# New order tables for the five engines of a one-core decoder layer

## The reference

```python
x = x + _L0_attn_ref(_layernorm(x, axis=-1), Wq, bq, Wk, bk, Wv, bv, Wo, bo)      # causal, with ALiBi
x = x + _L0_xattn_ref(_layernorm(x, axis=-1), ctx_1024, ctx_1024, ...)            # cross attention
x = x + _L0_ffn_ref(_layernorm(x, axis=-1), weight, aux_weight1, aux_weight2, bias)
# attention: softmax(q k^T / 4 + bias) v, then the output projection
# ffn: tanh(h @ weight @ aux_weight1 @ aux_weight2 + bias)
```

## Time and profile before

| | |
|---|---|
| median of 3 runs | 2504.38 us (2502.93 to 2504.84) |
| profiled execution | 2503.5 us, its span 2501.8 us |
| PE, busy of the span | 2335.8 us (93%) |
| PEld | 1856.7 us (74%) |
| DVE / ACT / POOL | 1700.1 (68%) / 1384.2 (55%) / 717.8 us (29%) |
| granted TensorE clock, mean | 0.984 |
| DMA | 244.83 MB, mean 98 GB/s |

### The profile page before, as it was taken

How to read it: one execution, slowest core, us unless ns; L and a number is a source line. 1 busy time by engine, 2 the same in 40 slices (tenths; PEclk the granted TensorE clock), 3 DMA queues, 4 the chain that set the end, 5 groups by cost and what they waited for, 6 DMA issues and landing times.

```text
span 2501.8 us, 67273 instructions
## 1 busy us (share of the span) xinstructions
PE 2335.8 (93%) x22072; PEld 1856.7 (74%) x22072; DVE 1700.1 (68%) x3710; ACT 1384.2 (55%) x3066; POOL 717.8 (29%) x1371
## 2 busy tenths in 40 slices
PE   4799999999999999999999999999999999999995
PEld 3677777777777777777777777777777777777763
DVE  4477667767767767767767767776776776776752
ACT  2455555565565555555555555556556556556551
POOL 3132233233233233233222223223223323323321
PEclk9899999999999999999999999999999999999995
DMA  8333433443343343333343343344344334334320
GB/s 157 88 101 96 110 97 85 107 112 86 104 112 83 101 106 93 105 103 85 101 107 93 101 107 93 89 107 104 90 107 105 85 100 113 92 100 109 86 69 21
DMA packets 167370, 244.83 MB, mean 98 GB/s; under 512 B 22176, under 2 KB 90512, under 8 KB 164248
## 3 DMA queue, kind: packets, MB, share of 16 engines
q1 hardware_dynamic: 165660, 244.22, 37.4%
q10 hardware_dynamic: 1664, 0.01, 0.1%
HBM read 53.13 MB, written 33.56 MB: 35 GB/s over the span
## 4 chain that ended last, share of the span: by engine, by line
PE 53%; DVE 11%; DMA 10%; issue 9%; ACT 8%; POOL 4%; SPq 4%; ACTq 0%; DVEq 0%; POOLq 0%
PE ps_misc L540 14%; PE ps_score L614 7%; PE ps_misc L526 6%; PE ps_attend L639 5%; DMA k_stack<-k_nat 5%; DMA q_stack<-neg_max_t_s 5%; DVE neg_max_s L954 4%; PE ps_misc L669 4%; PE ps_misc L510 3%; PE ps_score L615 3%; PE ps_max L597 3%; ACT xprobs L804 3%; PE ps_score L624 2%; DVE chain_t L937 2%; PE ps_attend L643 2%
## 5 line engine op out<-in xcount | busy, mean ns | idle before, releaser
L797 ACT ACTIVATE probs<-ps_score 128x384 f32<-128x384 f32 x1024 | 468.6, 494 | 113.3 <-PE ps_score L615 111.1
L954 DVE TENSOR_REDUCE neg_max_s<-ps_max 128x2 f32<-128x512 f32 (+1 forms) x768 | 478.7, 678 | 8.4 <-PE ps_max L585 4.4
L804 ACT ACTIVATE xprobs<-ps_score 120x512 f32<-120x512 f32 x512 | 280.7, 603 | 222.9 <-PE ps_score L624 222.8
L1080 POOL TENSOR_SCALAR ve_LN<-mv_LN 128x2 f32<-128x2 f32 x192 | 36.8, 191 | 1213.6 <-DVE mv_LN L976 1213.6
L614 PE MATMUL ps_score<-q_stack,k_stack 128*128 128x256 f32 x1024 | 353.2, 351 | 27.6 <-DMA q_stack<-neg_max_t_s 13.9
L962 DVE TENSOR_REDUCE neg_max_x<-ps_max 128x4 f32<-128x480 f32 x512 | 313.8, 649 | 61.1 <-PE ps_max L597 61.1
L615 PE MATMUL ps_score<-q_stack,k_stack 128*128 128x256 f32 x1024 | 283.8, 281 | 0.0
L614 PEld LDWEIGHTS ps_score<-q_stack,k_stack 128*128 128x128 f32 x1024 | 193.9, 189 | 109.3 <-ACT probs L797 47.1
L624 PE MATMUL ps_score<-xq_stack,xk_stack 128*120 128x256 f32 x1024 | 228.6, 316 | 6.6 <-DMA xq_stack<-neg_max_t_x 2.8
L1106 POOL TENSOR_TENSOR res<-res,chain_n 128x512 f32<-128x512 f32 x64 | 82.5, 1288 | 442.9 <-ACT chain_n L842 442.9
L597 PE MATMUL ps_max<-xk_stack,xq_stack 127*128 127x120 bf16 x2048 | 195.3, 220 | 1.2 <-DVE neg_max_x L962 1.2
(11 more groups left out here) (147 smaller groups left out, 5365.2 us busy)
## 6 DMA issues: line engine op xcount, KB each, us to landing
k_stack<-k_nat SPq DMA_DIRECT2D x192, 256.0 KB, 3.6
q_stack<-q_nat SPq DMA_DIRECT2D x192, 256.0 KB, 3.7
xq_stack<-q_nat SPq DMA_DIRECT2D x192, 256.0 KB, 3.6
xk_stack<-scr_xk SPq DMA_DIRECT2D x192, 128.0 KB, 2.9
x_in<-in_x SPq DMA_DIRECT2D x64, 256.0 KB, 2.8
scr_xk<-k_nat SPq DMA_DIRECT2D x32, 512.0 KB, 3.4
out_y<-res SPq DMA_DIRECT2D x64, 256.0 KB, 2.2
ctx_in<-in_ctx SPq DMA_DIRECT2D x32, 240.0 KB, 4.1
```

The lines of the kernel that those rows point to most:

```text
L797: act.activation(probs[:, h % 8, :], bank_of("SCORE", i, b, h)[:, P:4 * P], ACT.Exp)\
L804: act.activation(xprobs[0:C, at:at + 2, :], blocks(bank_of("XSCORE", i, b, u))[0:C], ACT.Exp).then_inc(sem("xprobs_ready"), 1)
L954: dve.tensor_reduce(o, ins, AX.X, ALU.max, negate=True).then_inc(sem("max_taken"), 1)
```

## The change

New tables for SP, PE, ACT, DVE and POOL in ORDER. They hold the same tasks, begun at another point of the cycle (PE's old table begins at SCORE 11 of the sequence in self attention, the new one at SCORE 4), with some moved: XK, XQ, LN2_T, V, XMAX, MAX, FFN and OUT_PROJ among others. Three functions follow: after_first is called on each engine before its first task that comes_first doesn't name, and no longer at t == 0; the wait of other_weights on PE covers all tasks done before it; and XHEADS_OUT of the last sequence on DVE waits for out_ready (cross_free). END_STEP is one lower.

```diff
--- before.py
+++ after.py
@@ -64,51 +64,50 @@
 
 ORDER = {
     "SP": (
-        ("STORE", -3, 0), ("XMAX_STACK", -2, 0), ("LOAD_X", 1, 0), ("XK_STACK", -1, 0),
-        ("MAX_STACK", 0, 0), ("XQ_STACK", -1, 0), ("LOAD_CTX", 0, 0),
-        ("K_STACK", 1, 0), ("Q_STACK", 1, 0), ("XK_SAVE", 0, 0),
+        ("LOAD_X", 1, 0), ("MAX_STACK", 0, 0), ("XK_STACK", -1, 0), ("LOAD_CTX", 0, 0),
+        ("XQ_STACK", -1, 0), ("K_STACK", 1, 0), ("Q_STACK", 1, 0), ("XMAX_STACK", -1, 0),
+        ("STORE", -2, 0), ("XK_SAVE", 0, 0),
     ),
     "PE": (
-        ("SCORE", -1, 11), ("ATTEND", -1, 1), ("SCORE", -1, 12), ("SCORE", -1, 13),
-        ("LN3_T", -3, 0), ("XMAX", -2, 3), ("ATTEND", -1, 2), ("SCORE", -1, 14), ("XMAX", -2, 4),
-        ("SCORE", -1, 15), ("XMAX", -2, 5), ("FFN", -3, 0), ("ATTEND", -1, 3), ("XMAX", -2, 6),
-        ("V", 0, 0), ("XMAX", -2, 7), ("HEADS_OUT", -1, 0), ("HEADS_OUT", -1, 1), ("MAX", 0, 0),
-        ("XMAX_T", -2, 0), ("MAX", 0, 1), ("OUT_T", -1, 0), ("MAX", 0, 2), ("XV", -1, 0),
-        ("MAX", 0, 3), ("MAX", 0, 4), ("MAX", 0, 5), ("OUT_PROJ", -1, 0), ("XSCORE", -2, 0),
-        ("XSCORE", -2, 1), ("MAX", 0, 6), ("MAX", 0, 7), ("XSCORE", -2, 2), ("MAX", 0, 8),
-        ("XSCORE", -2, 3), ("XATTEND", -2, 0), ("XSCORE", -2, 4), ("MAX", 0, 9), ("XSCORE", -2, 5),
-        ("XATTEND", -2, 1), ("MAX", 0, 10), ("XSCORE", -2, 6), ("MAX", 0, 11), ("XSCORE", -2, 7),
-        ("LN2_T", -1, 0), ("MAX_T", 0, 0), ("XATTEND", -2, 2), ("XATTEND", -2, 3), ("XQ", -1, 0),
-        ("SCORE", 0, 0), ("SCORE", 0, 1), ("XHEADS_OUT", -2, 0), ("SCORE", 0, 2),
-        ("XHEADS_OUT", -2, 1), ("SCORE", 0, 3), ("LN1_T", 1, 0), ("SCORE", 0, 4), ("XOUT_T", -2, 0),
-        ("ATTEND", 0, 0), ("SCORE", 0, 5), ("K", 1, 0), ("SCORE", 0, 6), ("XOUT_PROJ", -2, 0),
-        ("SCORE", 0, 7), ("SCORE", 0, 8), ("CTX_T", 0, 0), ("Q", 1, 0), ("SCORE", 0, 9),
-        ("XMAX", -1, 0), ("SCORE", 0, 10), ("XMAX", -1, 1), ("XK", 0, 0), ("XMAX", -1, 2),
+        ("SCORE", 0, 4), ("ATTEND", 0, 0), ("SCORE", 0, 5), ("XOUT_T", -2, 0), ("SCORE", 0, 6),
+        ("K", 1, 0), ("SCORE", 0, 7), ("SCORE", 0, 8), ("XOUT_PROJ", -2, 0), ("SCORE", 0, 9),
+        ("Q", 1, 0), ("XMAX", -1, 0), ("SCORE", 0, 10), ("SCORE", 0, 11), ("XMAX", -1, 1),
+        ("ATTEND", 0, 1), ("SCORE", 0, 12), ("XMAX", -1, 2), ("CTX_T", 0, 0), ("SCORE", 0, 13),
+        ("XMAX", -1, 3), ("XMAX", -1, 4), ("XMAX", -1, 5), ("SCORE", 0, 14), ("LN3_T", -2, 0),
+        ("XMAX", -1, 6), ("SCORE", 0, 15), ("XK", 0, 0), ("XMAX", -1, 7), ("ATTEND", 0, 2),
+        ("FFN", -2, 0), ("XMAX_T", -1, 0), ("MAX", 1, 0), ("MAX", 1, 1), ("ATTEND", 0, 3),
+        ("MAX", 1, 2), ("MAX", 1, 3), ("MAX", 1, 4), ("HEADS_OUT", 0, 0), ("MAX", 1, 5),
+        ("HEADS_OUT", 0, 1), ("XSCORE", -1, 0), ("XSCORE", -1, 1), ("MAX", 1, 6), ("XV", 0, 0),
+        ("OUT_T", 0, 0), ("XATTEND", -1, 0), ("XSCORE", -1, 2), ("XSCORE", -1, 3), ("MAX", 1, 7),
+        ("MAX", 1, 8), ("MAX", 1, 9), ("XSCORE", -1, 4), ("OUT_PROJ", 0, 0), ("MAX", 1, 10),
+        ("XSCORE", -1, 5), ("XSCORE", -1, 6), ("MAX", 1, 11), ("XATTEND", -1, 1), ("XSCORE", -1, 7),
+        ("V", 1, 0), ("MAX_T", 1, 0), ("XATTEND", -1, 2), ("XATTEND", -1, 3), ("LN2_T", 0, 0),
+        ("XHEADS_OUT", -1, 0), ("SCORE", 1, 0), ("SCORE", 1, 1), ("XHEADS_OUT", -1, 1),
+        ("SCORE", 1, 2), ("SCORE", 1, 3), ("XQ", 0, 0), ("LN1_T", 2, 0),
     ),
     "ACT": (
-        ("SCORE", -1, 11), ("ATTEND", -1, 1), ("SCORE", -1, 12), ("SCORE", -1, 13),
-        ("LN3_T", -3, 0), ("SCORE", -1, 14), ("SCORE", -1, 15), ("FFN", -3, 0), ("ATTEND", -1, 3),
-        ("V", 0, 0), ("XMAX_T", -2, 0), ("OUT_T", -1, 0), ("XSCORE", -2, 0), ("XSCORE", -2, 1),
-        ("XV", -1, 0), ("XSCORE", -2, 2), ("XSCORE", -2, 3), ("XSCORE", -2, 4), ("XSCORE", -2, 5),
-        ("XATTEND", -2, 1), ("XSCORE", -2, 6), ("XSCORE", -2, 7), ("LN2_T", -1, 0), ("MAX_T", 0, 0),
-        ("XATTEND", -2, 3), ("XQ", -1, 0), ("SCORE", 0, 0), ("SCORE", 0, 1), ("SCORE", 0, 2),
-        ("SCORE", 0, 3), ("LN1_T", 1, 0), ("SCORE", 0, 4), ("XOUT_T", -2, 0), ("K", 1, 0),
-        ("SCORE", 0, 5), ("SCORE", 0, 6), ("CTX_T", 0, 0), ("SCORE", 0, 7), ("SCORE", 0, 8),
-        ("Q", 1, 0), ("SCORE", 0, 9), ("SCORE", 0, 10), ("XK", 0, 0),
+        ("XSCORE", -2, 7), ("MAX_T", 0, 0), ("V", 0, 0), ("XATTEND", -2, 3), ("LN2_T", -1, 0),
+        ("SCORE", 0, 0), ("SCORE", 0, 1), ("SCORE", 0, 2), ("SCORE", 0, 3), ("XQ", -1, 0),
+        ("LN1_T", 1, 0), ("SCORE", 0, 4), ("SCORE", 0, 5), ("XOUT_T", -2, 0), ("SCORE", 0, 6),
+        ("K", 1, 0), ("SCORE", 0, 7), ("SCORE", 0, 8), ("SCORE", 0, 9), ("Q", 1, 0),
+        ("SCORE", 0, 10), ("SCORE", 0, 11), ("SCORE", 0, 12), ("CTX_T", 0, 0), ("SCORE", 0, 13),
+        ("ATTEND", 0, 1), ("SCORE", 0, 14), ("LN3_T", -2, 0), ("SCORE", 0, 15), ("XK", 0, 0),
+        ("XMAX_T", -1, 0), ("FFN", -2, 0), ("ATTEND", 0, 3), ("XSCORE", -1, 0), ("XSCORE", -1, 1),
+        ("XV", 0, 0), ("OUT_T", 0, 0), ("XSCORE", -1, 2), ("XSCORE", -1, 3), ("XSCORE", -1, 4),
+        ("XSCORE", -1, 5), ("XSCORE", -1, 6), ("XATTEND", -1, 1),
     ),
     "DVE": (
-        ("XMAX", -2, 2), ("XMAX", -2, 3), ("LN3_T", -3, 0), ("FFN", -3, 0), ("XMAX", -2, 4),
-        ("XMAX", -2, 5), ("XMAX", -2, 6), ("XMAX", -2, 7), ("HEADS_OUT", -1, 0),
-        ("HEADS_OUT", -1, 1), ("MAX", 0, 0), ("MAX", 0, 1), ("MAX", 0, 2), ("OUT_T", -1, 0),
-        ("MAX", 0, 3), ("MAX", 0, 4), ("MAX", 0, 5), ("OUT_PROJ", -1, 0), ("LN2", -1, 0),
-        ("MAX", 0, 6), ("MAX", 0, 7), ("MAX", 0, 8), ("MAX", 0, 9), ("MAX", 0, 10), ("MAX", 0, 11),
-        ("LN2_T", -1, 0), ("LN1", 1, 0), ("XQ", -1, 0), ("XHEADS_OUT", -2, 0),
-        ("XHEADS_OUT", -2, 1), ("LN1_T", 1, 0), ("XOUT_T", -2, 0), ("K", 1, 0),
-        ("XOUT_PROJ", -2, 0), ("LN3", -2, 0), ("CTX_T", 0, 0), ("Q", 1, 0), ("XMAX", -1, 0),
-        ("XMAX", -1, 1), ("XK", 0, 0),
+        ("MAX", 0, 3), ("HEADS_OUT", -1, 0), ("HEADS_OUT", -1, 1), ("MAX", 0, 4), ("MAX", 0, 5),
+        ("MAX", 0, 6), ("OUT_T", -1, 0), ("MAX", 0, 7), ("MAX", 0, 8), ("MAX", 0, 9),
+        ("OUT_PROJ", -1, 0), ("LN2", -1, 0), ("MAX", 0, 10), ("MAX", 0, 11), ("LN1", 1, 0),
+        ("LN2_T", -1, 0), ("XHEADS_OUT", -2, 0), ("XHEADS_OUT", -2, 1), ("XQ", -1, 0),
+        ("LN1_T", 1, 0), ("XOUT_T", -2, 0), ("K", 1, 0), ("XOUT_PROJ", -2, 0), ("LN3", -2, 0),
+        ("XMAX", -1, 0), ("Q", 1, 0), ("XMAX", -1, 1), ("XMAX", -1, 2), ("XMAX", -1, 3),
+        ("CTX_T", 0, 0), ("XMAX", -1, 4), ("XMAX", -1, 5), ("LN3_T", -2, 0), ("XMAX", -1, 6),
+        ("XMAX", -1, 7), ("XK", 0, 0), ("FFN", -2, 0), ("MAX", 1, 0), ("MAX", 1, 1), ("MAX", 1, 2),
     ),
     "POOL": (
-        ("LN3", -3, 0), ("FFN", -3, 0), ("LN2", -1, 0), ("LN1", 1, 0),
+        ("FFN", -2, 0), ("LN2", 0, 0), ("LN1", 2, 0), ("LN3", -1, 0),
     ),
 }
 
@@ -133,7 +132,7 @@
 for _k in ("LN1_T", "Q", "K", "V", "MAX_T", "OUT_T", "OUT_PROJ", "LN2_T", "XQ", "XMAX_T",
            "XOUT_T", "XOUT_PROJ", "LN3_T", "FFN", "CTX_T", "XK", "XV"):
     FILLS[_k] = ("misc", 1)
-FIRST_STEP, LOOP_FROM, LOOP_TO, END_STEP = -2, 6, 62, NSEQ + 3
+FIRST_STEP, LOOP_FROM, LOOP_TO, END_STEP = -2, 6, 62, NSEQ + 2
 
 
 def bank_turns():
@@ -294,15 +293,23 @@
                     wait(eng, name, per, i, b0, p0 + 1)
             return banks[FILLS[kind][0]][bank]
 
+        def comes_first(kind, b):
+
+            return kind in ("LOAD_X", "LOAD_CTX", "LN1", "LN1_T", "K", "Q") or \
+                kind in ("K_STACK", "Q_STACK") and b == 0
+
         def walk(eng, name, do, after_first):
 
             def step(i, t):
                 for kind, b, part in step_order(name, t):
                     do[kind](i, b, part)
+            waiting = True
             for t in range(FIRST_STEP, LOOP_FROM):
-                if t == 0:
-                    after_first()
-                step(0, t)
+                for kind, b, part in step_order(name, t):
+                    if waiting and not comes_first(kind, b):
+                        after_first()
+                        waiting = False
+                    do[kind](0, b, part)
             with eng.Fori(0, (LOOP_TO - LOOP_FROM) // 2) as i:
                 for t in range(LOOP_FROM, LOOP_FROM + 2):
                     step(i, t)
@@ -483,13 +490,14 @@
 
             def other_weights():
 
+                first = [(k, b) for t in range(FIRST_STEP, LOOP_FROM) for k, b, _ in step_order("PE", t)]
+                first = first[:[comes_first(k, b) for k, b in first].index(False)]
                 pe.wait_ge(sem("w_loaded_f2"), 16)
                 for n, nm in enumerate(REST):
                     if n == 0:
-                        pe.wait_ge(sem("K_lo"), 1)
-                    elif n == 1:
-                        pe.wait_ge(sem("Q_lo"), 1)
-                    else:
+                        for kind, b in first:
+                            pe.wait_ge(sem(GIVEN_BACK[kind][0]), b + 1)
+                    elif n > 1:
                         pe.wait_ge(sem("prep_lo"), len(FIRST) + n - 1)
```

(9 more changed lines are left out.)

## The result

The changed kernel takes 2414.91 us in the median of 4 runs (2413.22 to 2416.9), the kernel before 2504.61 us (2502.93 to 2505.15). The ratio is 0.9644, with a 95% interval of 0.9632 to 0.9656: faster by 3.6%, about 90 us. The forecast was 2438 us, so the sign and the cause held and the gain was 23 us larger than worked out.

What follows compares the result with a forecast made beforehand. The prediction took PE's row of tasks with short waits to bound the kernel. Head 91.8, 63 steps of 35.7 and tail 94.1 gave a span of 2435.0 us, forecast as 2438 us, with a range of 2400 to 2500 us.

Steps and rivals of the forecast that it cites:

- The first rival: Loop: only idle PE, 1.33 us a step, can be won; halved, the step is 36.5 and the time 2488 us; chance 0.14.
- The loop, 35.7: Each of 63 steps takes 35.7 us instead of 37.15, with ends of 35.1 and 36.5; gain 91 us.
- The floor of 32.8: Loop: PE's tasks of one step, added at their start-to-start distances where no wait is shown, take 32.8 us.
- the laid stalls of 2.4: Loop: waits of PE worked out for the new order, 0.15 + 1.1 + 0.35 + 0.5 + 0.3 = 2.4 us a step.
- the allowance of 0.5 for small pieces: Loop: 0.5 us a step added for small stalls that laying misses, taken between none and 1.3.
- One step that was wrong: XK: Loop: XK behind SCORE 15 takes off a stall of every second step, and SCORE 12's with it, 0.2 to 0.3 us.
- The head, 91.8: Head: SCORE 0 of sequence 0 starts at 91.8 us instead of 65.1, a cost of 26.7 us.
- the chain: Head: LN1 of sequence 1 ends at 64.6, zeroing to 75.0, row DMAs to 88.8, then 3.05 us from MAX_STACK to SCORE 0.
- The tail: Tail: five more XMAX tasks may run while LN3_T waits for POOL; 2 us come off, between 0 and 4.
- The slower one: Loop: cross queries land too late for XMAX 0 and Q; with 2.2 us late, 2539 us; chance 0.06.
- the head would be hidden: Head: its delay is hidden, giving 2411 us; chance 0.03.
- the tables do nothing in the loop: Loop: the stall before SCORE 0 eats the other gains; step stays 37.15 and the head's cost remains, 2529 us; chance 0.07.

Runs made afterwards that it cites:

- experiment 5: Changed kernel with the edit of experiment 1, and XV moved from behind MAX 6 to behind XATTEND 3 on PE and ACT: 2369.14 us, ratio 0.9454.
- experiment 2: Changed kernel with V moved back from before MAX_T to behind MAX 4 on PE, and behind ATTEND 3 on ACT: 2532.64 us, ratio 1.0113.
- experiment 3: Changed kernel with XQ moved back ahead of SCORE 0, behind XHEADS_OUT 0 on PE, ACT and DVE following: 2500.04 us, ratio 0.998.
- experiment 4: Kernel before with XK alone moved behind SCORE 15 on PE and ACT, behind LN3_T on DVE, and XK_SAVE behind XMAX_STACK: 2501.49 us, ratio 0.9984.
- experiment 1: Changed kernel with LN1 coming first for sequence 0 alone, so POOL zeroes the tiles right after LN1 of sequence 0: 2389.35 us, ratio 0.9542.
- experiment 9: Changed kernel with XMAX 0 moved from behind Q to ahead of it, on PE alone: 2486.92 us, ratio 0.9928.

## Why the prediction was right, and where it was off

**What bounds it.** Right: each step is PE's row of tasks with short waits, and a table can take them off with no instruction changed. The first rival, that only idle PE can be won, fell. The idle of PE was 80.4 us in 60.5 steps, 1.33 a step; it is now (2161.00 - 2098.02)/61.25 = 1.03. It gave 0.3 us a step, while 1.87 came off. The rest stood in rows as busy time: the busy time of the matmuls fell from 35.8 to 34.3 us a step with the same instructions, while that of the weight loads stayed at 28.5. Here the Trainium skill, Perfetto Trace Analysis, section Identifying the Most-Contended Engine, is borne out by the trace, in that the load's share is the better measure: PE's busy share rose only from 96.4% to 97.1%, while the share of the weight loads rose from 76.8% (1726.37/2247) to 80.8% (1746.57/2161), by 5%, like the pace of the steps. The overlap that I gave as the page's reason is what the rows show (0.28 us long, 0.12 apart); the page says that pipelined instructions look smaller in the trace, and here the matmuls' busy time is the larger figure, as it holds waits too.

**The loop, 35.7 against 35.28.** The floor of 32.8 and the laid stalls of 2.4 give 35.2, and the loop takes 35.28. By difference, the allowance of 0.5 for small pieces that a laying by hand misses was too large by 0.4. That is 63 x 0.42 = 26.5 us, more than the whole error. It is a balance of larger errors, though, and that they cancel so well is luck: by the spacings the seven projections take 10.3 us and not 10.5, and OUT_T, OUT_PROJ and K hardly wait (0.3 laid), while the eight XMAX take 2.0 and not 1.6, and the twelve MAX 2.9, where 2.2 and a stall of 0.5 were counted.

The laid pieces in turn. MAX_T to SCORE 0 was to be stalled by 1.1 and is by 1.15, and for the reason given: the maxima take 3.2 us from MAX_T to their landing (3.1 said), and SCORE 0 starts as they land. The wait for POOL's layer norm ahead of LN2_T, 0.82 of the 1.15 by the spacings, was not foreseen, but it lies inside this time; experiment 5 shows it, as 0.78 us of XV there change nothing. MAX_T was to wait 0.15 and hardly waits (V's spacing is 1.48, XQ's 1.44); experiment 2 shows that without V it is 1.4. MAX 3 and 4 were to wait 0.5 together and wait 0.3: the spacing ahead of MAX 3 is 0.24 where a free one is 0.15, and ahead of MAX 4 it is 0.45 against 0.21. XQ waits for nothing, as said; at its old place it would wait 0.88 us a step in the new table (experiment 3).

**One step that was wrong: XK.** I said that with XK behind SCORE 15 a stall of every second step goes, and SCORE 12's with it, 0.2 to 0.3 us. SCORE 12's did (0.50 to 0.35), but experiment 4 shows that the move alone gives next to nothing, as SCORE 11 then waits for its exp. In the new table Q stands between SCORE 9 and 10 and may give the exps that time; this was not tried by itself.

**The head, 91.8 against 97.2.** Its cause is shown by experiment 1. The links of the chain held: three memsets 10.4 us, the issue of the rows 13.6 (13.7 said), and the 2.7 us that V's departure gives (from the start of DVE's last weight task to the first MAX 0.75 us instead of 3.48). V took so long there because the granted clock was 0.50 (the last section). What I missed is that the chain starts later. The turning of the other weights on PE starts at 43.26 instead of 38.20:

```profile
43.26 0.45 PE L481 MATMUL ps_misc<-chain_n,xprobs 128*128 128x256 f32 x1 [1.93 <-DVE q_nat L945]
```

Of these 5.06 us, 1.93 are this wait: other_weights now waits on PE for all that was done before it. It stands in the diff, and I had costed it at nothing without naming its cover. Another 0.63 is the pace of the K and Q matmuls, which the last section puts down to the clock. The last 2.50 are not the change's: LN1 of sequence 0 starts on POOL at 30.15 instead of 27.66, behind input that lands later; it starts at 30.32 in experiment 1, 31.85 in 5, and in experiment 4, which is the kernel before with XK moved, at 32.13. The first line is of the kernel before, the second of the changed one:

```profile
27.66 0.19 POOL L1080 TENSOR_SCALAR ve_LN<-mv_LN 128x2 f32<-128x2 f32 x1 [20.81 <-DVE mv_LN L976]
30.15 0.19 POOL L1095 TENSOR_SCALAR ve_LN<-mv_LN 128x2 f32<-128x2 f32 x1 [23.29 <-DVE mv_LN L984]
```

The last link was 0.5 too short too: 3.58 us from MAX_STACK to SCORE 0.

**The tail.** Predicted -2 (0 to 4), measured -4.5. Counted from SCORE 0 of sequence 63, the first of its eight XMAX tasks starts at 44.5 us in the kernel before and the last at 57.0, with LN3_T and FFN of the last but one sequence between them. Now they start between 45.7 and 49.6 us: six (24 matmuls) in one row ahead of LN3_T, behind a wait for the cross queries that the prediction did not have, and two behind it.

```profile
2365.45 3.05 PE L605 MATMUL ps_max<-xk_stack,xq_stack 127*128 127x120 bf16 x24 [2.68 <-DMA xq_stack<-q_nat]
```

XMAX_T comes 6.2 us earlier by this. Of these, 1.1 us are the clock and not the order: FFN there runs at a granted clock of 1.00 now and at 0.50 before (1.4 us from its first to its last matmul, and 2.5). Up to the last XATTEND 1.7 us go back, and 4.5 remain to the end.

**The rivals.** The slower one did not come, but its mechanism is real and near: 0.3 us of slack, and a cost of nearly one to one behind it (experiment 9). The prediction had a slack of 0.6. It took 3.6 us from issue to landing, which is the middle of all 192 transfers, while the one that is waited for is the last of three, with 4.0. In the changed kernel it lands 7.6 us after XQ's last matmul, of the 8.06 us to XMAX 0. The whole gain is 90.4/63 = 1.43 us a step; with the slack, the queries would have to land 1.7 us later to turn the sign. That the head would be hidden, and that the tables do nothing in the loop, fell by the first two rows of the table.
